# Relation rows in the first graph layer: from a per-edge gather to a one-hot matrix product

## The chip, the cores and the metric

The program runs on one core of one Trainium2 chip. Each core has TensorE (PE) for matrix products, VectorE (DVE), ScalarE (ACT), GpSimd (POOL), SyncE (SP), an on-chip memory of 128 partitions (SBUF), eight accumulation banks (PSUM) and sixteen DMA engines. The metric is device time in microseconds for one launch; lower is better.

## The reference

Two graph layers of a relational network and one graph transformer layer run over 50000 nodes and 25000 edges, all in float32 with 128 features. The change touches only the first of these layers:

```python
def _layer(h, e_h, src, dst, iso_mask, norm, W_r, W_sl, W_el):
    self_msg = jnp.where(iso_mask[:, None], h @ W_el, h @ W_sl)
    msg = (e_h + h[src]) @ W_r
    agg = jax.ops.segment_sum(msg, dst, num_segments=h.shape[0])
    return rrelu(agg * norm + self_msg)
...
e_h = rel_embed[rel_id]          # 25000 x 128, from a table of 200 rows
h = ent_embed
for W_r, W_sl, W_el in [(W_r1, W_sl1, W_el1), (W_r2, W_sl2, W_el2)]:
    h = _layer(h, e_h, src, dst, iso_mask, norm, W_r, W_sl, W_el)
```

The edges come sorted by `dst`. After the two layers follow a layer norm, an attention layer over the same edges and a feed-forward part over all nodes.

## The kernel before

The kernel is a row of stages, each a program of its own for every engine, with a barrier between two stages. `prepare` makes masks and index columns from the edge lists. `dense` runs over all nodes in 98 groups of 512 (NG = 98) and computes both layers for a node without edges; edges are corrected after it. `layer(0)` and `layer(1)` run over the edges in 49 groups of 512 (GE = 49), each of four tiles of 128 edges (GT = 4, T = 196 tiles). Then come `attention`, `softmax`, `weighted` and `ffn`.

Inside a stage every engine steps through the same counter `n`, and an operation with lag `a` works in step `n` on group `n - a`; semaphores do the rest. Each engine takes its instructions strictly in the order in which they are written.

**`dense`.** In step `n` SP issues the stores of older groups, then waits for the gather of pair `m = n - 5`, stores it to `edge_x` (L566), and only then loads `x_in` for group `n` (L571). POOL issues for each `m` two indirect DMAs of 128 rows of `x` (L538, `x_dst`, a ring of 8) and two of 128 rows of the relation table (L542) into `e_h`, a buffer of 196 tiles that stays in SBUF until the end of `layer(1)`. DVE does per step the two leaky maxima (L705, L756), the sum (L727), the norm's statistics, and its half of a search for the source positions (L689, every second step also L748). ACT evacuates PSUM (L647, L652, L657, L662), normalises three of four rows (L672) and counts signs (L637).

**`layer(0)`.** POOL gathers four tiles of source rows per group (L874, `h_src`, a ring of 6 groups). With A = 4, DVE first waits for all relation rows, then adds in step `n` the group's relation rows and source rows (`msg`, L955, group `n - 5`), takes the leaky maximum (L963, group `n - 8`), and alternates four `accT` (L1002, group `n - 6`) with four `mate` (L1011, group `n - 5`). PE does per step `p_acc` (L892, 4 products, group `n - 6`), `p_own` (L902, 4 transposes) and `p_h` (L911 and L912, 8 products, group `n - 7`). `layer(1)` gathers from `h1_table` and uses `e_h` directly as an operand of `p_acc` (L894).

Of the kernel before, what the change touches and what calls it, by code (L numbers as in the profile page):

```python
# [5 lines left out]
F32 = mybir.dt.float32  # L6
# [8 lines left out]
P = 128  # L15
# [12 lines left out]
SEG, FROM_PREV, TO_NEXT = range(3)  # L28
KINDS = 3
# [29 lines left out]
def gnn_program(nc, x, src, dst, edge_type_200, L0_gnn_rel_embed, L0_gnn_W_r1, L0_gnn_W_sl1, L0_gnn_W_el1,  # L59
# [18 lines left out]
    EDGES = GE * GROUP  # L78

# [11 lines left out]
    with root:  # L91
# [38 lines left out]
        types_in = sem("types_in", root)  # L130
# [36 lines left out]
        idx = sb("idx", [P, 6, T], I32)  # L167
        SRC, DST, AT_END, H_SRC, X_SRC, TYPE = range(6)
# [16 lines left out]
        def prepare():  # L185

            with ExitStack() as c:
# [14 lines left out]
                type_f = sb("type_f", [Q, W], F32, c)  # L202
# [54 lines left out]
                def _(e):  # L257
# [5 lines left out]
                    e.iota(row_id[:], pattern=[[1, 1]], base=0, channel_multiplier=1).then_inc(filled, 1)  # L263
                    e.memset(ident[:], 0.0).then_inc(consts, 1)
# [20 lines left out]
                def _(e):  # L285
                    e.wait_ge(filled, 6)
# [15 lines left out]
                    e.wait_ge(weights_in, 6 * 16)  # L302
# [20 lines left out]
                def _(e):  # L323
# [13 lines left out]
                    for n, t in enumerate((src_f, dst_in, end_f, seg_f, done_t, type_f)):  # L337
                        to_columns(n, t)
# [16 lines left out]
                def _(e):  # L355
# [13 lines left out]
                    e.tensor_copy(type_f[:], type_i[:])  # L369
# [77 lines left out]
                    e.wait_ge(turned, 6)  # L447
                    for n, t in ((0, idx[:, SRC, :]), (0, src_col[:]), (1, idx[:, DST, :]), (2, idx[:, AT_END, :]), (3, seg_col[:]), (5, idx[:, TYPE, :])):
# [10 lines left out]
                    e.wait_ge(turned, 7)  # L459
# [3 lines left out]
        def dense(e_h):  # L463

            XN, PN, SN = 16, 8, 4
            with ExitStack() as c:
# [67 lines left out]
                def _(e):  # L534
                    for m in range(NG):
# [246 lines left out]
        def layer(l, e_h):  # L782

            RN, HN, ON = 8, 6, 8
            with ExitStack() as c:
                rows = sb("rows", [P, RN, 2, 2 * W], U8, c)
                h_src = sb("h_src", [P, HN, GT, D], F32, c)
# [15 lines left out]
                p_h = [ps(f"p_h{s}", c) for s in range(2)]  # L803
                rows_in = sems("rows_in", RN, c)
# [20 lines left out]
                src_used = msg_ready if l == 0 else acc_prod  # L825
# [10 lines left out]
                def row_of(g, j, kind):  # L836
                    return tile_row(rows[:, g % RN, :, :], j, kind)

                @block.sync
                def _(e):  # L840
                    for n in range(STEPS):
# [7 lines left out]
                        if at_step(n, 0):  # L849
# [3 lines left out]
                            e.dma_start(rows[:, g % RN, :, :], edge_row(g, SEG, FROM_PREV + 1)).then_inc(rows_in[g % RN], 16)  # L853
# [15 lines left out]
                def _(e):  # L869
                    for g in range(GE):  # L870
                        wait(e, src_used, g - HN + 1)
                        for j in range(GT):
                            t = g * GT + j
                            e.indirect_dma_start(out=h_src[:, g % HN, j, :], out_offset=None, in_=(x, h1_table)[l],  # L874
                                                 in_offset=bass.IndirectOffsetOnAxis(ap=idx[:, (SRC, H_SRC)[l], t:t + 1], axis=0))\
# [3 lines left out]
                def _(e):  # L879
                    for n in range(STEPS):  # L880
# [23 lines left out]
                        if at_step(n, A + 3):  # L904
# [8 lines left out]
                            mm.then_inc(h_prod, 1)  # L913

                @block.scalar
                def _(e):
                    for n in range(STEPS):
                        if at_step(n, A + 2):
# [3 lines left out]
                            e.activation(ownT[:, g % 2, :], p_own[g % 2][:], ACT.Copy).then_inc(ownT_ready, 1)  # L922
                        if l and at_step(n, A + 8):
# [889 lines left out]
```

## Time and profile before

| | |
|---|---|
| median of 3 runs | 2668.84 us (2665.56 to 2669.47) |
| span of the profiled execution, first to last instruction | 2664.4 us |
| mean granted TensorE clock | 0.915 of full speed |
| instructions | 47955 |
| busy: PE, DVE, ACT, POOL | 2108.4, 1957.4, 1283.9, 1426.5 us |
| mean DMA rate | 159 GB/s |

The profiled execution's own time is not reported apart from its span: the span lies 1.2 us under the lowest and 5.1 us under the highest of the three runs, so between 1 and 5 us pass outside it. A busy share over the whole span mixes eight stages; the rows below are therefore cut by stage. `dense` runs from about 44 to 561 us, `layer(0)` from 564 to 830 us, `layer(1)` from 831 to about 1130 us, and `ffn` holds the last 740 us.

### The profile page before, as it was taken

Reading aid. Unit: us, or ns where it says so; the run is one execution under the profiler, and the core shown is the slowest. Engines: PE = TensorE matmul, PEld = TensorE weight load, DVE = VectorE, ACT = ScalarE, POOL = GpSimd, SP = SyncE. Lnnn points to the kernel's source line nnn. Section 1 sums busy time; section 2 is a strip of 40 time slices with the busy share of each in tenths; the row PEclk is TensorE's granted clock in tenths of the full one; section 3 lists DMA queues with packets and bytes.
Section 4 is the critical chain, followed back from the end, with each engine's and each line's share of the span. In section 5 each row is a group of like instructions: output and inputs, shape, how many; then the busy total and the mean of one; then the engine's idle time right before and its main releaser. Section 6 shows DMA issues by size and latency. Waiting matters only on the chain. (4 is left out here: it accounts for less than half of the span.)

```text
span 2664.4 us, 47955 instructions
## 1 busy us (share of the span) xinstructions
PE 2108.4 (79%) x13630; PEld 1693.7 (64%) x13630; DVE 1957.4 (73%) x7853; ACT 1283.9 (48%) x3019; POOL 1426.5 (54%) x1595
## 2 busy tenths in 40 slices
PE   3777777747776777669999607888299999999998
PEld 3555555537776777657777505666177777777776
DVE  4888888866665777878888685676377777777774
ACT  2788888842211444546565310000156666666665
POOL 2777777757775776275553004777533333333332
PEclk9899998878888999979999758999599999999999
DMA  3788888866666999744443005565313333333331
GB/s 90 218 247 243 240 241 238 239 191 181 180 177 186 298 292 290 231 137 128 124 122 108 30 0 152 177 194 188 148 60 108 108 103 109 105 106 107 106 105 51
DMA packets 378875, 423.36 MB, mean 159 GB/s; under 512 B 54686, under 2 KB 263274, under 8 KB 378614
## 3 DMA queue, kind: packets, MB, share of 16 engines
q1 hardware_dynamic: 334774, 337.16, 40.6%
q0 software_dynamic: 40768, 82.23, 11.8%
q8 instruction: 111, 1.82, 0.3%
q10 hardware_dynamic: 3072, 0.92, 0.2%
q14 instruction: 150, 1.23, 0.1%
HBM read 273.64 MB, written 179.87 MB: 170 GB/s over the span
## 5 line engine op out<-in xcount | busy, mean ns | idle before, releaser
L1670 PEld LDWEIGHTS p_y<-w,g_T 128*128 128x128 f32 x3136 | 365.4, 192 | 46.4 <-issue 24.2
L1670 PE MATMUL p_y<-w,g_T 128*128 128x128 f32 x3136 | 365.8, 275 | 0.0
L1653 POOL TENSOR_TENSOR rstd<-var,minus_half 128x4 f32<-128x4 f32 x98 | 113.5, 1159 | 450.3 <-ACT res L1701 450.2
L1663 PE MATMUL p_f<-nT,w 128*128 128x512 f32 x784 | 354.3, 595 | 0.0
L1688 ACT ACTIVATE nT<-p_n 128x512 f32<-128x512 f32 x98 | 58.5, 597 | 577.0 <-PE p_n L1678 577.0
L1695 ACT ACTIVATE g_T<-p_f,bf 128x512 f32<-128x512 f32 x392 | 267.1, 681 | 31.4 <-PE p_f L1663 31.3
L1083 POOL DMA_INDIRECT x_src<-x_rows,idx x196 | 185.1, 944 | 166.2 <-DVE normed L1250 73.6
L1488 POOL DMA_INDIRECT x_rows<-xv,idx x196 | 210.5, 1074 | 86.2 <-issue 53.1
L538 POOL DMA_INDIRECT x_dst<-in_x_dram,idx x196 | 197.1, 1005 | 100.5 <-issue 100.5
L874 POOL DMA_INDIRECT h_src<-h_table,idx x196 | 190.1, 970 | 87.7 <-issue 55.2
L1663 PEld LDWEIGHTS p_f<-nT,w 128*128 128x128 f32 x784 | 142.0, 191 | 141.7 <-issue 141.7
L874 POOL DMA_INDIRECT h_src<-in_x_dram,idx x196 | 190.5, 972 | 75.9 <-issue 58.8
L939 ACT ACTIVATE low<-p_h 128x512 f32<-128x512 f32 x98 | 58.5, 597 | 341.5 <-PE p_h L912 341.5
L542 POOL DMA_INDIRECT e_h<-in_L_gnn_rel_embed_dram,idx x196 | 187.0, 954 | 59.7 <-issue 59.7
L1717 DVE TENSOR_TENSOR xs<-p_y,xs 128x512 f32<-128x512 f32 x98 | 67.8, 692 | 184.8 <-PE p_y L1670 184.8
L1701 ACT ACTIVATE res<-xs,shift,rstd 128x128 f32<-128x128 f32 x392 | 189.3, 487 | 4.7 <-DVE shift L1756 4.7
L615 PE MATMUL p_r<-ident,h1T 128*128 128x128 f32 x392 | 67.1, 296 | 122.4 <-ACT h_rows L652 122.4
L911 PE MATMUL p_h<-w_r,accT 128*128 128x128 f32 x784 | 163.7, 293 | 0.0
L912 PE MATMUL p_h<-w_sl,ownT 128*128 128x128 f32 x784 | 161.4, 290 | 0.0
L608 PEld LDWEIGHTS p<-w_el,h1T 128*128 128x128 f32 x784 | 107.6, 203 | 71.9 <-DVE h1T L756 41.1
L1011 DVE TENSOR_SCALAR mate<-rows,seg_col,norm_col 128x128 f32<-128x128 uint8 x392 | 141.1, 363 | 10.2 <-DMA rows<-edge_rows 10.0
L1002 DVE SCALAR_TENSOR_TENSOR accT<-rows,accT,p_acc 128x128 f32<-128x128 uint8 x390 | 132.2, 339 | 12.6 <-PE p_acc L892 7.5
(298 smaller groups left out, 5683.5 us busy)
## 6 DMA issues: line engine op xcount, KB each, us to landing
xs<-x_rows SPq DMA_DIRECT2D x98, 512.0 KB, 3.6
x_in<-in_x_dram SPq DMA_DIRECT2D x98, 256.0 KB, 3.6
h_table<-h_rows SPq DMA_DIRECT2D x98, 256.0 KB, 3.9
x_rows<-x_in SPq DMA_DIRECT2D x98, 256.0 KB, 4.4
out_dram<-res SPq DMA_DIRECT2D x98, 256.0 KB, 2.1
x_rows<-x_rows SPq DMA_DIRECT2D x50, 500.0 KB
rows<-edge_rows SPq DMA_DIRECT2D x147, 128.0 KB, 4.5
edge_x<-x_dst SPq DMA_DIRECT2D x98, 128.0 KB, 2.2
```

The lines of the kernel that those rows point to most:

```text
L538: e.indirect_dma_start(out=x_dst[:, m % PN, j, :], out_offset=None, in_=x, in_offset=bass.IndirectOffsetOnAxis(ap=idx[:, DST, 2 * m + j:2 ...
L542: e.indirect_dma_start(out=e_h[:, t, :], out_offset=None, in_=L0_gnn_rel_embed, in_offset=bass.IndirectOffsetOnAxis(ap=idx[:, TYPE, t:t + ...
L874: e.indirect_dma_start(out=h_src[:, g % HN, j, :], out_offset=None, in_=(x, h1_table)[l], in_offset=bass.IndirectOffsetOnAxis(ap=idx[:, (S ...
L911: e.matmul(p_h[g % 2][:, at], accT[:, g % 2, at], w_r[l][:], start=True, stop=False)
L912: mm = e.matmul(p_h[g % 2][:, at], ownT[:, g % 2, at], w_sl[l][:], start=False, stop=True)
L1011: ins = e.tensor_scalar(mate[:, g % 2, j * P:(j + 1) * P], row_of(g, j, SEG), seg_col[:, t:t + 1], norm_col[:, t:t + 1], ALU.is_equal, ALU ...
L1083: e.indirect_dma_start(out=x_src[:, k % SN, j, :], out_offset=None, in_=x_rows, in_offset=bass.IndirectOffsetOnAxis(ap=idx[:, X_SRC, t:t + ...
L1488: e.indirect_dma_start(out=both_table.rearrange("n a d -> n (a d)"), in_=xv[:, g % VN, j, :, :].rearrange("p a d -> p (a d)"), in_offset=None,
L1663: e.matmul(p_f[ch][:], w_1[:, ch * P:(ch + 1) * P], nT[:, g % 2, :], start=True, stop=True).then_inc(f_prod, 1)
L1670: mm = e.matmul(p_y[g % 2][:, a * D:(a + 1) * D], g_T[:, g % 2, ch, a * P:(a + 1) * P], w_2[:, ch, :], start=(ch == 0), stop=(ch == FCH - 1))
L1695: e.activation(g_T[:, g % 2, ch, :], p_f[ch][:], ACT.Gelu, bias=bf1[:, ch:ch + 1]).then_inc(gelu_ready, 1)
L1701: ins = e.activation(res[:, g % RN, ch, :], xs[:, g % XN, ch, X1, :], ACT.Identity, scale=rstd2[:, g % 2, ch:ch + 1], bias=shift2[:, g % 2 ...
```

## The change

The relation rows are no longer gathered. `prepare` loads the table of 200 rows into SBUF (`rel`, two halves of 128 rows, the second padded with zeros) and writes each edge's type as a byte into `edge_rows`, as a fourth kind, instead of turning it into an index column. In `layer(0)` DVE compares the type bytes of 512 edges, spread over all partitions, with the row number of each partition, once for each half of the table (`onehot`, two instructions of 128x512). PE multiplies these with `rel` (8 products of 128x128 for a group) into two new PSUM banks `p_rel`. `msg` adds `p_rel` to the source rows, and ACT copies `p_rel` into `e_h`, which `layer(1)` needs.

The source rows of `layer(0)` are gathered into `e_h` itself, at the places which the relation rows take later, instead of into a ring of six groups. The first six groups' source rows (24 indirect DMAs) are gathered in `dense`; the other 43 groups' in `layer(0)`, up to 10 groups ahead of `msg`. The 196 relation gathers in `dense` are gone.

```diff
-SEG, FROM_PREV, TO_NEXT = range(3)
-KINDS = 3
+TYPE, SEG, FROM_PREV, TO_NEXT = range(4)
+KINDS = 4
...
+                    e.iota(rel_i[:], pattern=[[P, 2]], base=0, channel_multiplier=1).then_inc(filled, 1)
+                    e.memset(rel[:], 0.0).then_inc(filled, 1)
...
-                    e.wait_ge(filled, 6)
+                    e.wait_ge(filled, 8)
...
+                    e.dma_start(rel[:, 0, :], L0_gnn_rel_embed[0:P, :]).then_inc(weights_in, 16)
+                    e.dma_start(rel[0:RELS - P, 1, :], L0_gnn_rel_embed[P:RELS, :]).then_inc(weights_in, 16)
...
-                    e.tensor_copy(type_f[:], type_i[:])
+                    e.tensor_copy(rows[:, TYPE, :], type_i[:])
+                    e.tensor_copy(rel_id[:], rel_i[:])
...
-                    for n, t in ((0, idx[:, SRC, :]), (0, src_col[:]), (1, idx[:, DST, :]), (2, idx[:, AT_END, :]), (3, seg_col[:]), (5, idx[:, TYPE, :])):
+                    for n, t in ((0, idx[:, SRC, :]), (0, src_col[:]), (1, idx[:, DST, :]), (2, idx[:, AT_END, :]), (3, seg_col[:])):
...
-                        for t in (2 * m, 2 * m + 1):
-                            e.indirect_dma_start(out=e_h[:, t, :], out_offset=None, in_=L0_gnn_rel_embed,
-                                                 in_offset=bass.IndirectOffsetOnAxis(ap=idx[:, TYPE, t:t + 1], axis=0))\
-                                .then_inc(types_in, 16)
+                        if m < EARLY * GT:
+                            e.indirect_dma_start(out=x_src[:, m, :], out_offset=None, in_=x,
+                                                 in_offset=bass.IndirectOffsetOnAxis(ap=idx[:, SRC, m:m + 1], axis=0))\
+                                .then_inc(early_in, 16)
...
+            AHEAD = HN if l else 10
...
+                            if l == 0:
+                                wait(e, onehot_ready, g - RN + 1)
+                            e.dma_start(rows[:, g % RN, :, :], edge_row(g, FIRST, FROM_PREV + 1)).then_inc(rows_in[g % RN], 16)
...
+                    if l == 0:
+                        for g in range(EARLY, GE):
+                            k = g - EARLY
+                            if k >= AHEAD:
+                                e.wait_ge(msg_ready, g - AHEAD + 1)
+                            for t in range(g * GT, (g + 1) * GT):
+                                e.indirect_dma_start(out=e_h[:, t, :], out_offset=None, in_=x,
+                                                     in_offset=bass.IndirectOffsetOnAxis(ap=idx[:, SRC, t:t + 1], axis=0))\
+                                    .then_inc(gathered[k % AHEAD], 16)
+                        return
...
+                        if l == 0 and at_step(n, A):
+                            g = n - A
+                            e.wait_ge(onehot_ready, g + 1)
+                            wait(e, rel_ready, g - 1)
+                            for j in range(GT):
+                                at = slice(j * P, (j + 1) * P)
+                                for half in range(2):
+                                    mm = e.matmul(p_rel[g % 2][:, at], onehot[:, g % 2, half, at], rel[:, half, :],
+                                                  start=(half == 0), stop=(half == 1))
+                            mm.then_inc(rel_prod, 1)
...
+                        if l == 0 and at_step(n, A + 1):
+                            g = n - A - 1
+                            e.wait_ge(rel_prod, g + 1)
+                            e.wait_ge(msg_ready, g + 1)
+                            e.activation(e_h[:, g * GT:(g + 1) * GT, :].rearrange("p j d -> p (j d)"), p_rel[g % 2][:], ACT.Copy)\
+                                .then_inc(rel_ready, 1)
...
-                        e.wait_ge(types_in, 16 * T)
+                        e.wait_ge(early_in, 16 * EARLY * GT)
...
+                        if l == 0 and at_step(n, A):
+                            g = n - A
+                            e.wait_ge(rows_in[g % RN], 16 * (g // RN + 1))
+                            wait(e, rel_prod, g - 1)
+                            for half in range(2):
+                                ins = e.tensor_scalar(onehot[:, g % 2, half, :].rearrange("p (q i) -> p q i", q=2),
+                                                      rows[:, g % RN, :, 0:W], rel_id[:, half:half + 1], None, ALU.is_equal)
+                            ins.then_inc(onehot_ready, 1)
...
-                            e.wait_ge(gathered[g % HN], gathered.after(g % HN, GT * (g // HN + 1)))
+                            e.wait_ge(rel_prod, g + 1)
+                            if g >= EARLY:
+                                k = g - EARLY
+                                e.wait_ge(gathered[k % AHEAD], gathered.after(k % AHEAD, GT * (k // AHEAD + 1)))
...
-                            e.tensor_tensor(msg[:, g % 2, :, :].rearrange("p j d -> p (j d)"),
-                                            e_h[:, g * GT:(g + 1) * GT, :].rearrange("p j d -> p (j d)"),
-                                            h_src[:, g % HN, :, :].rearrange("p j d -> p (j d)"), ALU.add).then_inc(msg_ready, 1)
+                            e.tensor_tensor(msg[:, g % 2, :, :].rearrange("p j d -> p (j d)"), p_rel[g % 2][:],
+                                            e_h[:, g * GT:(g + 1) * GT, :].rearrange("p j d -> p (j d)"), ALU.add).then_inc(msg_ready, 1)
```

PE does its new products last in a step, DVE its new compares first. The `rows` DMA of `layer(0)` brings three kinds instead of two. `layer(1)` and all later stages keep their instructions.

## Rows read from the trace of the kernel before

**Rows 1.** The chain that ended last, by engine

```profile
PE 27%; DVE 0%; ACT 0%; DMA 0%; issue 0%; ACTq 0%
```

**Rows 2.** Busy us of each engine by stretch, mean granted clock, DMA share

```profile
core 0: us, PE busy (x) PEld busy (x) DVE busy (x) ACT busy (x) POOL busy (x), PEclk, DMA share, GB/s
44.00:556.00 512.00, 369.98 (x2548) 286.91 (x2548) 430.50 (x1958) 418.33 (x1170) 384.02 (x392) 0.92 0.79 234
100.00:500.00 400.00, 291.78 (x2025) 226.38 (x2026) 342.23 (x1560) 333.30 (x934) 305.22 (x312) 0.93 0.81 240
564.00:830.00 266.00, 191.46 (x1372) 184.37 (x1372) 165.87 (x490) 53.42 (x98) 190.53 (x196) 0.86 0.61 170
600.00:800.00 200.00, 151.19 (x1086) 146.34 (x1086) 131.38 (x391) 42.34 (x78) 152.19 (x157) 0.87 0.64 179
831.00:1130.00 299.00, 220.63 (x1764) 211.32 (x1764) 224.78 (x980) 135.78 (x339) 190.11 (x196) 0.93 0.91 279
2000.00:2300.00 300.00, 300.00 (x1782) 223.48 (x1782) 228.20 (x1008) 182.72 (x363) 106.07 (x161) 1.00 0.33 106
```

**Rows 3.** POOL's groups of instructions, 100 to 500 us: busy, mean ns, idle before

```profile
L538 POOL DMA_INDIRECT x_dst<-in_x_dram,idx x156 | 157.2, 1008 | 47.5 <-issue 47.5
L542 POOL DMA_INDIRECT e_h<-in_L_gnn_rel_embed_dram,idx x156 | 149.2, 957 | 47.5 <-issue 47.5
```

**Rows 4.** Waits of SP's queue, 100 to 500 us: us in total, times, longest

```profile
SPq L566 <- DMA x_dst<-in_x_dram,idx: 224.5, 73, 5.4
SPq L561 <- ACT x_in L672: 3.8, 4, 1.5
```

**Rows 5.** Waits of ACT, PE and DVE, 100 to 500 us

```profile
PE p_r L615 <- ACT h_rows L652: 106.0, 65, 4.1
ACT h_rows L652 <- DMA h_table<-h_rows: 57.6, 47, 3.2
DVE base L687 <- ACT junk L637: 20.1, 33, 1.7
DVE h L705 <- DVE junk L689: 17.5, 78, 0.6
DVE h1T L756 <- ACT low L657: 17.2, 18, 2.1
```

**Rows 6.** POOL's three groups of gathers, 44 to 830 us

```profile
L538 POOL DMA_INDIRECT x_dst<-in_x_dram,idx x196 | 197.1, 1005 | 100.5 <-issue 100.5
L874 POOL DMA_INDIRECT h_src<-in_x_dram,idx x196 | 190.5, 972 | 75.9 <-issue 58.8 <-POOLq L120 16.4 <-DVE msg L955 0.6
L542 POOL DMA_INDIRECT e_h<-in_L_gnn_rel_embed_dram,idx x196 | 187.0, 954 | 59.7 <-issue 59.7
```

**Rows 7.** The msg line L955 in the first layer: duration, first and last start, waits

```profile
L955 DVE TENSOR_TENSOR msg<-e_h,h_src x49: 678/693/766, 574.3 to 816.7; 128x512 f32<-128x512 f32 x49
its engine sat idle before it (us, times) until:
  DMA h_src<-in_x_dram,idx: 88.8, 30
```

**Rows 8.** Timeline of DVE, two steps at 300 us: start, us

```profile
299.99 0.69 DVE L705 TENSOR_TENSOR h<-low,p 128x512 f32<-128x512 f32 x1 [0.21 <-DVE junk L689]
302.63 0.65 DVE L748 TENSOR_SCALAR at_least<-srcs,first_col 98x512 bf16<-98x512 uint16 x2
304.89 0.69 DVE L705 TENSOR_TENSOR h<-low,p 128x512 f32<-128x512 f32 x1 [0.21 <-DVE junk L689]
```

**Rows 9.** Timeline of DVE at 542 us, a step without L748

```profile
542.52 0.69 DVE L705 TENSOR_TENSOR h<-low,p 128x512 f32<-128x512 f32 x1 [0.21 <-DVE junk L689]
...
546.78 0.69 DVE L705 TENSOR_TENSOR h<-low,p 128x512 f32<-128x512 f32 x1 [0.21 <-DVE junk L689]
```

**Rows 10.** DVE's L705, once for each of the 98 groups of the dense stage

```profile
L705 DVE TENSOR_TENSOR h<-low,p x98: 679/687/690, 58.4 to 549.4; 128x512 f32<-128x512 f32 x98
```

**Rows 11.** A float32 instruction of DVE at 128x512, in prepare

```profile
L456 DVE TENSOR_SCALAR w<-w,gcol x1: 481/481/481, 41.9 to 41.9; 128x512 f32<-128x512 f32 x1
```

**Rows 12.** Timeline of PE at 709 us; a float32 product is two records

```profile
709.15 1.06 PE L892 MATMUL p_acc<-mate,msg 128*128 128x128 f32 x8
710.04 0.60 PE L902 MATMUL p_own<-ident,h_own 128*128 128x128 f32 x4
710.48 0.28 PE L911 MATMUL p_h<-w_r,accT 128*128 128x128 f32 x1
```

**Rows 13.** Timeline of DVE, one step of the first layer without a wait

```profile
700.88 0.69 DVE L955 TENSOR_TENSOR msg<-e_h,h_src 128x512 f32<-128x512 f32 x1 [3.20 <-DMA h_src<-in_x_dram,idx]
701.50 0.68 DVE L963 TENSOR_TENSOR out_rows<-low,p_h 128x512 f32<-128x512 f32 x1
702.09 0.34 DVE L1002 SCALAR_TENSOR_TENSOR accT<-rows,accT,p_acc 128x128 f32<-128x128 uint8 x1
702.35 0.34 DVE L1011 TENSOR_SCALAR mate<-rows,seg_col,norm_col 128x128 f32<-128x128 uint8 x1
...
704.15 0.69 DVE L955 TENSOR_TENSOR msg<-e_h,h_src 128x512 f32<-128x512 f32 x1
```

**Rows 14.** The two-byte compare L748: shortest, median, longest ns

```profile
L748 DVE TENSOR_SCALAR at_least<-srcs,first_col x98: 322/347/551, 48.2 to 531.1; 98x512 bf16<-98x512 uint16 x98
```

**Rows 15.** The rows DMA, 556 to 700 us: issue, then time to landing

```profile
L853 SPq DMA_DIRECT2D rows<-edge_rows x31: 370/380/454, 563.8 to 695.7; - x31
DMA to landing us min/median/max: 3.1/4.6/6.8
```

**Rows 16.** SP's issues at the start of the first layer

```profile
563.79 0.39 SPq L853 DMA_DIRECT2D rows<-edge_rows  x1
564.23 0.46 SPq L856 DMA_DIRECT2D h_own<-edge_x  x1
```

**Rows 17.** Timeline of PE at 822 us, at the low clock

```profile
822.39 0.64 PE L912 MATMUL p_h<-w_sl,ownT 128*128 128x128 f32 x2
822.81 0.63 PE L911 MATMUL p_h<-w_r,accT 128*128 128x128 f32 x2
823.24 0.63 PE L912 MATMUL p_h<-w_sl,ownT 128*128 128x128 f32 x2
```

More of the change, by code:

```diff
@@ L78, in gnn_program @@
     EDGES = GE * GROUP
+    RELS = L0_gnn_rel_embed.shape[0]
+    assert P < RELS <= min(2 * P, BYTE)
+    EARLY = 6
     h1_table = nc.dram_tensor("h1_table", [N + EDGES, D], F32).ap()
@@ L166, in gnn_program @@
         bf2_rows = sb("bf2_rows", [P, D])
-        idx = sb("idx", [P, 6, T], I32)
-        SRC, DST, AT_END, H_SRC, X_SRC, TYPE = range(6)
+        idx = sb("idx", [P, 5, T], I32)
+        SRC, DST, AT_END, H_SRC, X_SRC = range(5)
+        rel = sb("rel", [P, 2, D])
+        rel_id = sb("rel_id", [P, 2])
         src_col = sb("src_col", [P, T])
@@ L336, in _ @@
                     e.wait_ge(cols_ready, 1)
-                    for n, t in enumerate((src_f, dst_in, end_f, seg_f, done_t, type_f)):
+                    for n, t in enumerate((src_f, dst_in, end_f, seg_f, done_t)):
                         to_columns(n, t)
@@ L458, in _, with dense @@
                     e.tensor_copy(att_bias[:], p_att[:, 0:D])
-                    e.wait_ge(turned, 7)
+                    e.wait_ge(turned, 6)
                     e.tensor_copy(by_half(done_col[:]), columns(4))
                     e.tensor_copy(by_half(norm_col[:]), columns(6))
-        def dense(e_h):
+        def dense(x_src):
             XN, PN, SN = 16, 8, 4
@@ L784, in layer @@
             RN, HN, ON = 8, 6, 8
+            FIRST = SEG if l else TYPE
+            AHEAD = HN if l else 10
             with ExitStack() as c:
-                rows = sb("rows", [P, RN, 2, 2 * W], U8, c)
-                h_src = sb("h_src", [P, HN, GT, D], F32, c)
+                rows = sb("rows", [P, RN, 2, (FROM_PREV + 1 - FIRST) * W], U8, c)
+                h_src = sb("h_src", [P, HN, GT, D], F32, c) if l else None
+                onehot = None if l else sb("onehot", [P, 2, 2, GROUP], F32, c)
                 h_own = sb("h_own", [P, HN, GT, D], F32, c)
@@ L803, in layer @@
                 p_h = [ps(f"p_h{s}", c) for s in range(2)]
+                p_rel = None if l else [ps(f"p_rel{s}", c) for s in range(2)]
+                onehot_ready = None if l else sem("onehot_ready", c)
+                rel_prod = None if l else sem("rel_prod", c)
+                rel_ready = None if l else sem("rel_ready", c)
                 rows_in = sems("rows_in", RN, c)
@@ L824, in layer @@
                 row_ready = sem("row_ready", c) if l else h_ready
-                src_used = msg_ready if l == 0 else acc_prod
                 block = program(c)
@@ L836, in row_of @@
                 def row_of(g, j, kind):
-                    return tile_row(rows[:, g % RN, :, :], j, kind)
+                    return tile_row(rows[:, g % RN, :, :], j, kind - FIRST)
                 @block.sync
@@ L869, in _ @@
                 def _(e):
+                    if l == 0:
[8 more added lines that the diff above has]
+                        return
                     for g in range(GE):
-                        wait(e, src_used, g - HN + 1)
+                        wait(e, acc_prod, g - HN + 1)
                         for j in range(GT):
                             t = g * GT + j
-                            e.indirect_dma_start(out=h_src[:, g % HN, j, :], out_offset=None, in_=(x, h1_table)[l],
-                                                 in_offset=bass.IndirectOffsetOnAxis(ap=idx[:, (SRC, H_SRC)[l], t:t + 1], axis=0))\
+                            e.indirect_dma_start(out=h_src[:, g % HN, j, :], out_offset=None, in_=h1_table,
+                                                 in_offset=bass.IndirectOffsetOnAxis(ap=idx[:, H_SRC, t:t + 1], axis=0))\
                                 .then_inc(gathered[g % HN], 16)
```

11 lines of the change are left out of this document (5 added, 6 removed).

## The prediction

> **What bounds the kernel now.** The chain that ended last is first, and it says little here: it follows PE through `ffn` for 27% of the span and stops there [rows 1]. All stages touched lie before it, behind barriers, so whatever they gain or lose reaches the end in full. I therefore read stage by stage.
>
> The second view is busy time by stretch [rows 2]. In `dense` no engine is full: over 400 us DVE is busy for 342.23, ACT for 333.30, POOL for 305.22 and PE for 291.78, DMA at 0.81. In the middle of `layer(0)` all are lower still. Busy shares alone name no bound.
>
> The third view does: POOL's groups. Its 312 gathers between 100 and 500 us take 157.2 + 149.2 us and sit idle for 47.5 + 47.5 us, all "issue", so POOL waited for nobody: 401.4 us of 400 [rows 3]. That stretch holds 78 steps, so four gathers cost 5.15 us a step, and that is the pace of the stage. The fourth view shows how it reaches the others: SP's queue waits 224.5 us, 2.9 us a step, for the `x_dst` gather [rows 4]. SP takes its work in order, so the `h1_table` stores stand behind that wait; ACT then waits 57.6 us for those stores before `h_rows`, and PE 106.0 us for ACT [rows 5]. The reader is to see a gather that nobody reads soon setting the pace of a stage through an in-order queue.
>
> `layer(0)` has the same bound: 196 gathers, 190.5 us busy and 58.8 us of issue, 1.27 us each, 5.09 us a group [rows 6]; `msg` waits 88.8 us for them, and its 48 intervals from 574.3 to 816.7 are 5.05 us each [rows 7].
>
> **Dense, part by part.** Removed are 196 gathers, 187.0 + 59.7 us of POOL's time [rows 6]; 24 are added. POOL's step falls from four gathers to two (2.6 us), or three in the first 24 steps (3.9 us). It stops being the bound. What is late next is DVE: 342.23 us over 78 steps is 4.39 us [rows 2], and 17.5 us over 78 is 0.22 us a step of a wait on its own chain, in every step [rows 5], which stays: 4.61 us. Single steps agree: 4.90 us with L748 [rows 8] and 4.26 us without it [rows 9], mean 4.58 us. DVE's other two waits, 20.1 and 17.2 us on ACT [rows 5], are 0.48 us a step. If they came only from SP's stall they go; if ACT's own order makes them they stay, and nothing is gained. The ends are 4.61 and 5.06 us; the latter is today's mean interval, (549.4 - 58.4) / 97 [rows 10]. ACT needs 333.30 / 78 = 4.27 us and PE 3.74 us [rows 2], both under DVE, and DMA gets 128 KB a step less. I take 4.65. Gain: 97 x (5.06 - 4.65) = **-40 us**; ends -44 and 0.
>
> **Prepare** gets an iota, a memset and two more loads, all small, ahead of or beside a chain that loses one column turn and one copy. The nearest duration is the 0.48 us of a DVE instruction over the same 512 columns [rows 11]; I take **+0.4 us**, ends 0 and 2.
>
> **The first layer, PE.** Today a group has 4 products of `p_acc` in 0.89 us and 4 transposes in 0.44 us [rows 12]; a product is 0.222 us, so the 8 of `p_h` are 1.78 us. That is 3.11 us. The change adds 8 products, 1.78 us: 4.89 us a group. This becomes the longest queue of the stage.
>
> **DVE.** A step without waits is 3.27 us [rows 13]. The two compares are not in the trace as such. Below, each could be as cheap as the two-byte compare of as many columns, 0.33 us when two follow each other [rows 8, 14]; a float32 scalar instruction of 512 columns is 0.48 us [rows 11]. Above, one element a cycle like `msg` gives 0.69 us [rows 7], and four times a byte-reading `mate` gives 4 x 0.26 = 1.04 us [rows 13]. I take 0.6, nearest to `msg`, because the byte-reading `mate` is no shorter than the byte-reading `accT` with three operands. DVE: 3.27 + 1.2 = 4.5 us, hidden behind PE's 4.89; ends 3.9 and 5.35. Only at the upper end would DVE bound, at 48 x 0.3 = +14 us over today.
>
> **Order of the loop.** The new waits are DVE's `msg` on `rel_prod`, behind which stand the maximum, four `accT` and four `mate`, and ACT's copy on `msg_ready`, behind which stands `low`. PE ends step `n - 1` with `p_rel`; then DVE does `msg` and everything after it in 3.27 us, and PE needs that `mate` only at the start of its next step, 4.89 us later. So 1.6 us of slack remains, and the next compare fills most of it. PE needs the compare only at the end of its step. ACT gains one copy of 0.6 us beside 53.42 us of work in 266 [rows 2]: nothing. It holds `low` for the next step, where it is due.
>
> **POOL** in this stage: 43 groups at 5.09 us, starting with the first six resident, some 30 us ahead of need, with room for ten. At 5.0 us a group the lead shrinks by 43 x 0.09 = 4 us: covered. `rows` grows by half, 64 KB a group, at a DMA share of 0.64 [rows 2], and is loaded over three steps ahead of its compare against 4.6 us to land [rows 15]: nothing.
>
> **Start and loop.** Today `msg` starts 10.5 us after SP's first issue [rows 7, 16], waiting for gathers. New: 4.6 us landing, 1.3 us compares, 8 products at the low clock, 0.428 us each [rows 17], 3.4 us: 9.3 us, **-1 us**. The loop: 4.89 plus 0.1 us for semaphores is 5.0 us, 48 x (5.0 - 5.05) = **-2.4 us**. PE starts cold: while it stays at the low clock a step costs 9.8 us; with one and a quarter such steps **+6 us** (ends 0 and 12). The drain behind the last `msg` keeps its work: 0.
>
> **The clock.** In `layer(0)` the granted clock was 0.87 in mean with PE busy for 151.19 of 200 us, in `layer(1)` 0.93, and in `ffn`, where PE never paused, 1.00 [rows 2]. Those are mixtures of the levels 1.2 and 2.4 GHz. I expect near 1.0 because PE becomes the bound and stops pausing. The Trainium skill, "TensorE: Matmul & The Clock Gate", section "HAM oscillation", warns of the opposite: bursts of products between waits keep falling back to the low clock. By it, were the pauses to remain, the loop would come out as the second rival; the 0.87 row bears that rule out for the present loop.
>
> **Sum.** -40 + 0.4 - 1 - 2.4 + 6 = -37 us. Against the profiled span of 2664.4 that is 2627.4; between 1 and 5 us lie around the span, so against the median of 2668.84 it is 2632 us.
>
> **Rivals.** *Dense is freed only in part.* ACT's and DVE's waits on each other stay, or the gathers and stores contend: 4.90 us a step, -16 us, sum -13, 2656 us. For it: 37.3 us of DVE's waits are on ACT [rows 5]. Against: ACT and PE were themselves waiting for SP, and free steps of 4.26 and 4.90 us exist.
>
> *PE bounds the first layer at a mixed clock.* At 0.87 the loop is 4.89 / 0.87 + 0.1 = 5.7 us, 48 x 0.65 = +31 us in place of -2.4, sum -4, 2665 us. For it: today's clock rows. Against: `ffn`.
>
> *Slower than before.* One mechanism: PE waits in each step for `mate`, because DVE waits in each step for `p_rel`, so the two alternate instead of overlapping. PE from `p_acc` to `p_rel` is 4.89 us, then DVE 3.27 us: 8.2 us a step if the lag of one step were no cover. It decides from 5.05 + (40 - 5) / 48 = 5.8 us on; halfway, 6.6 us, it is 48 x 1.55 = +74 us, sum +40, 2709 us. Against it stand the two-step lag and the slack worked out above; for it, that a cold PE (9.8 us) eats all slack once and may stay so.
>
> *It doesn't do what it says in dense*: SP would wait for the x_dst gather as long as now, because landing and not issue is slow. 0 us there, sum about +3, 2672 us. Against: POOL's issues fill the stretch to within 1.4 us.
>
> **Numbers.** Forecast 0.63, dense in part 0.13, mixed clock 0.12, alternation 0.06, no gain in dense 0.06. A measurement tells about 0.2%, 5 us, from no change. The mixed clock splits evenly between faster and same, and partly freed dense counts as faster. Faster 0.82, same 0.07, slower 0.11. The range goes from -54 (dense 4.58, no cold start, PE at 4.89) to -12, which takes in dense in part: 2615 to 2657.
>
> **What would show it.** In the new profile POOL should be idle for over 40% of `dense`, with SP waiting for ACT or DVE and no longer for `x_dst`; L705's intervals near 4.6 us; `layer(0)` with PE busy over 90% at a clock over 0.95, `msg` waiting for PE and not for DMA, intervals near 5.0 us; the compares 0.5 to 0.7 us each. The prediction is wrong if L705's intervals stay over 4.9 us, if the clock in `layer(0)` stays under 0.9, or if the compare takes over 0.85 us.

## The result, and the profile after

The changed kernel takes 2598.63 us (median of 4 runs, 2596.22 to 2603.09); the kernel before, run beside it, 2669.15 us (2665.56 to 2671.54). The ratio is 0.9742, with a 95% interval of 0.9729 to 0.9755: 70 us faster. Predicted were 37 us, with a range that ended at 54. The direction was right, the size about half.

The profiled execution has a span of 2594.5 us, 69.9 us less than before. The first view is busy time by stretch: the middle of `dense`, the middle of `layer(0)`, `layer(1)`.

```profile
core 0: us, PE busy (x) PEld busy (x) DVE busy (x) ACT busy (x) POOL busy (x), PEclk, DMA share, GB/s
100.00:450.00 350.00, 262.08 (x1997) 197.49 (x1996) 330.02 (x1538) 326.01 (x924) 173.21 (x175) 1.00 0.85 246
550.00:750.00 200.00, 200.00 (x1797) 200.00 (x1796) 170.81 (x489) 68.85 (x123) 136.56 (x141) 1.00 0.66 185
761.00:1060.00 299.00, 225.12 (x1764) 215.87 (x1764) 224.86 (x980) 135.53 (x339) 190.10 (x196) 0.91 0.92 279
```

Beside [rows 2], in the middle of `dense` DVE is now busy for 94% of the time (86% before) and POOL for 49% (76%). In the middle of `layer(0)` PE has no gap at all, and its granted clock, 0.87 before, is 1.00. `layer(1)` takes as long as it did.

The second view is POOL's groups and the waits of SP's queue, 100 to 450 us, beside [rows 3] and [rows 4].

```profile
L548 POOL DMA_INDIRECT x_dst<-in_x_dram,idx x165 | 163.3, 990 | 173.8 <-DMA edge_x<-x_dst 142.5 <-issue 31.3
...
SPq L571 <- ACT x_in L682: 150.3, 77, 2.9
```

POOL now waits 142.5 us for `x_dst` buffers to come free, so it runs ahead of SP; SP no longer waits for a gather but for ACT.

The third view is DVE's L715 (L705 before), once a group, beside [rows 10], and two steps of its timeline, beside [rows 8] and [rows 9].

```profile
L715 DVE TENSOR_TENSOR h<-low,p x98: 679/687/690, 59.7 to 497.3; 128x512 f32<-128x512 f32 x98
...
300.23 0.69 DVE L715 TENSOR_TENSOR h<-low,p 128x512 f32<-128x512 f32 x1 [0.21 <-DVE junk L699]
304.48 0.69 DVE L715 TENSOR_TENSOR h<-low,p 128x512 f32<-128x512 f32 x1 [0.21 <-DVE junk L699]
307.12 0.61 DVE L758 TENSOR_SCALAR at_least<-srcs,first_col 98x512 bf16<-98x512 uint16 x2
309.27 0.69 DVE L715 TENSOR_TENSOR h<-low,p 128x512 f32<-128x512 f32 x1 [0.21 <-DVE junk L699]
```

97 intervals fell from 491.0 to 437.6 us, 5.06 to 4.51 us each. Two lengths alternate: 4.26 us, and 4.79 or some 4.93 us in a step with the two-byte compare (L758, L748 before). The 0.21 us wait on DVE's own chain stands in each, and in these steps DVE has no other.

The fourth view is two DVE lines of `layer(0)`, `msg` beside [rows 7] and the new compare, then DVE's timeline over one step.

```profile
L1010 DVE TENSOR_TENSOR msg<-p_rel,e_h x49: 684/692/692, 518.3 to 750.1; 128x512 f32<-128x512 f32 x49
its engine sat idle before it (us, times) until:
  PE p_rel L949: 33.8, 48
...
L995 DVE TENSOR_SCALAR onehot<-rows,rel_id x98: 468/482/636, 513.5 to 744.0; 128x512 f32<-128x512 uint8 x98
...
601.37 1.02 DVE L995 TENSOR_SCALAR onehot<-rows,rel_id 128x512 f32<-128x512 uint8 x2
603.01 0.69 DVE L1010 TENSOR_TENSOR msg<-p_rel,e_h 128x512 f32<-128x512 f32 x1 [0.62 <-PE p_rel L949]
603.62 0.68 DVE L1017 TENSOR_TENSOR out_rows<-low,p_h 128x512 f32<-128x512 f32 x1
607.91 0.69 DVE L1010 TENSOR_TENSOR msg<-p_rel,e_h 128x512 f32<-128x512 f32 x1 [0.28 <-PE p_rel L949]
```

`msg` waits for `p_rel` in nearly every step, 33.8 us in all, and for no gather: PE is the bound. The 48 intervals of `msg` take 231.8 us (242.4 before). A compare is 0.48 us.

Where the 69.9 us went, each figure a difference of starts in the two traces, rounded: the 97 intervals of `dense` -53.4; its tail from the last L715 to SP's first issue in `layer(0)` -2.1 (14.4 to 12.3); that issue to the first `msg` -1.8 (10.5 to 8.7); the 48 intervals of `msg` -10.6; the drain behind them -1.6 (13.9 to 12.3); `prepare` +1.0; `dense`'s start +0.3; `layer(1)` -1.5; all behind it -0.1.

### The profile page after: what moved, and what is told of

It is laid out like the page before. It is cut to its first block and busy times, and to the rows that moved or that the text cites. A ratio compares the mean times of both kernels' runs of the same rounds, so it can differ in the third digit from the quotient of the medians.

```text
span 2594.5 us, 49618 instructions
## 1 busy us (share of the span) xinstructions
PE 2131.5 (82%) x14412; PEld 1724.0 (66%) x14412; DVE 1990.0 (77%) x7951; ACT 1308.9 (50%) x3068; POOL 1238.0 (48%) x1401
## 3 DMA queue, kind: packets, MB, share of 16 engines
q0 software_dynamic: 34496, 69.37, 10.6%
## 5 line engine op out<-in xcount | busy, mean ns | idle before, releaser
L618 PEld LDWEIGHTS p<-w_el,h1T 128*128 128x128 f32 x784 | 95.1, 191 | 188.7 <-DVE h1T L766 187.8
L894 POOL DMA_INDIRECT e_h<-in_x_dram,idx x172 | 166.8, 970 | 104.6 <-POOLq L123 52.5
L618 PE MATMUL p<-w_el,h1T 128*128 128x128 f32 x784 | 113.2, 287 | 109.2 <-DVE h1T L766 109.2
L939 PE MATMUL p_h<-w_r,accT 128*128 128x128 f32 x784 | 152.5, 276 | 0.0
L940 PE MATMUL p_h<-w_sl,ownT 128*128 128x128 f32 x784 | 152.2, 276 | 0.0
L922 PE MATMUL p_acc<-mate,e_h 128*128 128x128 f32 x392 | 88.3, 310 | 56.9 <-DVE mate L1065 52.7
```

What stands on the lines that cost most here:

```text
L618: mm = e.matmul(p_2[g % 2][:, a * D:(a + 1) * D], h1T[:, g % 2, a * P:(a + 1) * P], w_el[1][:], start=True, stop=True)
L939: e.matmul(p_h[g % 2][:, at], accT[:, g % 2, at], w_r[l][:], start=True, stop=False)
L940: mm = e.matmul(p_h[g % 2][:, at], ownT[:, g % 2, at], w_sl[l][:], start=False, stop=True)
```

## Experiments

The four of the first series ask what set the pace of `dense`: POOL's time for issuing, or the traffic of the relation gathers. The next four ask what sets the pace of `layer(0)`, and what the six early groups are worth. The last three follow from those. Each series ran beside the kernel before; ratios are to it, and the changed kernel stands at 0.9742. The pace is the mean over all 97 intervals of `dense` or all 48 of `msg`, the short first and last ones among them.

| run | median us | ratio, 95% | pace per step of the stage it changes |
|---|---|---|---|
| dense alone | 2608.59 | 0.9796 (0.9776 to 0.9816) | dense 4.51 |
| gathers put back | 2654.30 | 0.9963 (0.9946 to 0.9980) | dense 5.07 |
| POOL kept busy | 2640.16 | 0.9924 (0.9899 to 0.9950) | dense 4.92 |
| traffic alone | 2599.17 | 0.9764 (0.9744 to 0.9783) | dense 4.50 |
| products twice | 2685.24 | 1.0077 (1.0059 to 1.0095) | layer(0) 6.60 |
| products halved | 2587.20 | 0.9709 (0.9689 to 0.9730) | layer(0) 4.56 |
| one early group | 2609.12 | 0.9795 (0.9778 to 0.9813) | layer(0) 5.04 |
| twelve early groups | 2599.47 | 0.9757 (0.9739 to 0.9774) | layer(0) 4.83 |
| bf16, two parts, twelve | 2561.54 | 0.9604 (0.9588 to 0.9620) | layer(0) 4.04 |
| bf16, three parts, twelve | 2581.01 | 0.9674 (0.9658 to 0.9690) | layer(0) 4.45 |
| bf16, two parts, six | 2583.41 | 0.9688 (0.9671 to 0.9704) | layer(0) 4.57 |

### The dense stage alone

The kernel before, with its relation gathers replaced by a memset; `layer(0)` as before.

```diff
-                        for t in (2 * m, 2 * m + 1):
-                            e.indirect_dma_start(out=e_h[:, t, :], out_offset=None, in_=L0_gnn_rel_embed,
...
+                        e.memset(e_h[:, 2 * m:2 * m + 2, :], 0.0).then_inc(types_in, 1)
```

> The kernel before without its 196 relation gathers in dense; a GpSimd memset of e_h to zero (0.3 us a step) stands in for them, so the relation rows are left out of the result. The first layer keeps its own gathers. Theory P (GpSimd's issue of four gathers a step set the pace of dense): dense falls from 5.06 to 4.5 us a step as in the changed kernel, 55 us less, about 2614 us, and the first layer's msg intervals stay 5.05 us. Rival L (a good part of the 70 us belongs to the first layer and to what it leaves behind): over 2630 us.

```profile
L702 DVE TENSOR_TENSOR h<-low,p x98: 680/686/689, 60.6 to 498.1; 128x512 f32<-128x512 f32 x98
...
L952 DVE TENSOR_TENSOR msg<-e_h,h_src x49: 678/692/749, 521.0 to 762.6; 128x512 f32<-128x512 f32 x49
```

`dense` runs at 4.51 us a step, as in the changed kernel, and `layer(0)` at 5.03 us, as before the change. The ratio of 0.9796 is -54 us of 2662; the changed kernel's 0.9742 is -69. The forecast on record was -55 us. So some 54 us of the gain are the gathers gone from `dense`, and the new first layer, with its early gathers, brings the other 14 or so.

### Gathers put back, POOL kept busy, traffic alone

Three additions to the changed kernel, 172 times each in `dense`, so that a step holds four operations again: a gather into buffer space not yet in use; a small POOL arithmetic instruction of about the same length that moves nothing; a plain transfer of the same size on SP's queue.

```diff
+                            e.indirect_dma_start(out=x_src[:, t, :], out_offset=None, in_=x,
+                                                 in_offset=bass.IndirectOffsetOnAxis(ap=idx[:, DST, t:t + 1], axis=0))\
+                                .then_inc(extra_in, 16)
...
+                            e.tensor_tensor(x_src[:, t, 0:5], pw_in[:], pw_half[:], ALU.pow).then_inc(extra_in, 1)
...
+                                e.dma_start(x_src[:, t, :], x[t * P:(t + 1) * P, :]).then_inc(extra_in, 16)
```

> The changed kernel with 172 gathers of node rows added to dense, into tiles of e_h that are not yet in use, so that GpSimd issues four gathers in each step as before. Their rows are overwritten later and change no result. Theory P: dense back to 5.06 us a step, +53 us, about 2652 us, with the first layer's loop at 4.90 us. Rival T (traffic): the same, so this run only fixes the size that the next two must share out.

> The changed kernel with two power operations of 128x5 on GpSimd in each dense step (one in the first 24), which take its time without any DMA; their results are overwritten. From the 1.16 us of a 128x4 power in ffn I expect 1.3 us each. Theory P: two gathers at 1.25 and two powers at 1.3 are about 5.1 us a step, dense back near 5.06 us, 2645 to 2665 us. Rival T (the relation gathers cost by their DMA traffic): dense stays at 4.5 us, 2600 us.

> The changed kernel with the same number of transfers of the same size and packet length (128 rows of 512 bytes) added to dense, issued by SyncE's queue and not by GpSimd; their rows are overwritten. Theory P: dense stays at 4.5 us a step, 2600 us, at most 5 us more for 0.8 us of issue a step on SyncE. Rival T: dense back near 5 us a step, 2640 to 2655 us.

The intervals of the same DVE line, in this order:

```profile
L724 DVE TENSOR_TENSOR h<-low,p x98: 679/686/690, 60.7 to 552.1; 128x512 f32<-128x512 f32 x98
```

```profile
L728 DVE TENSOR_TENSOR h<-low,p x98: 676/686/689, 59.0 to 536.4; 128x512 f32<-128x512 f32 x98
```

```profile
L722 DVE TENSOR_TENSOR h<-low,p x98: 677/686/689, 60.0 to 496.6; 128x512 f32<-128x512 f32 x98
```

And POOL's groups of the second, 59 to 537 us:

```profile
L566 POOL TENSOR_TENSOR e_h<-pw_in,pw_half 128x5 f32<-128x5 f32 x170 | 204.4, 1209 | 2.3
L556 POOL DMA_INDIRECT x_dst<-in_x_dram,idx x190 | 195.5, 1029 | 46.2 <-issue 46.1
L560 POOL DMA_INDIRECT e_h<-in_x_dram,idx x22 | 21.2, 964 | 6.7 <-issue 6.7
```

The numbers of that view add up to 476 us of 478: POOL is full, and `dense` takes 4.92 us a step without one relation row being moved. That is less than the 5.07 us with gathers, and the run's 2640.16 us lie under the 2645 to 2665 expected: two powers of 1.21 us and two gathers of 1.27 us with their issue gap make about 4.96 us, not 5.1. In the same kernel SP's queue waits again for the `x_dst` gather, 189.6 us between 100 and 450 us. With the traffic and without POOL's work the pace is 4.50 us, at a DMA share of 0.91 in the middle of the stage. The added transfers differ from the gathers in two ways, they come from SP's queue and read rows that lie together; scattered reads without POOL's work were not run. With that said, the relation gathers cost `dense` their time on POOL, and the same number of bytes alone costs nothing that can be measured.

### Products twice, products halved

PE's new products are done twice (the result is the same), or for the first half of the table alone.

```diff
-                                for half in range(2):
-                                    mm = e.matmul(p_rel[g % 2][:, at], onehot[:, g % 2, half, at], rel[:, half, :],
-                                                  start=(half == 0), stop=(half == 1))
+                                for half in range(4):
+                                    mm = e.matmul(p_rel[g % 2][:, at], onehot[:, g % 2, half % 2, at], rel[:, half % 2, :],
+                                                  start=(half % 2 == 0), stop=(half % 2 == 1))
...
-                                for half in range(2):
-                                    mm = e.matmul(p_rel[g % 2][:, at], onehot[:, g % 2, half, at], rel[:, half, :],
-                                                  start=(half == 0), stop=(half == 1))
+                                mm = e.matmul(p_rel[g % 2][:, at], onehot[:, g % 2, 0, at], rel[:, 0, :],
+                                              start=True, stop=True)
```

> The changed kernel with the 8 products of p_rel done twice for each group, the second time over the first. Theory E (TensorE sets the first layer's pace now, its products back to back at 0.222 us): the step grows by exactly 8 x 0.222 = 1.78 us to 6.68 us, 48 x 1.78 = +85 us, about 2683 us against 2598. Rival V (VectorE or the hand-over between the two sets the pace): part of the new products fills TensorE's waiting, +40 to +65 us.

> The changed kernel with only the first half of the relation table in the products (4 instead of 8 for a group; edges of types 128 to 199 get a zero row, so the result is another). Theory E: TensorE's step falls to 4.0 us and GpSimd's gathers become the bound: 43 groups at 5.07 us from 510 us on, the last row lands near 731 us where the last msg now starts at 750, so -19 us, about 2580 us. Rival V: VectorE or the hand-over holds the step at 4.9 us, no change.

`msg` with the products twice, and halved:

```profile
L1010 DVE TENSOR_TENSOR msg<-p_rel,e_h x49: 691/692/693, 521.5 to 838.1; 128x512 f32<-128x512 f32 x49
its engine sat idle before it (us, times) until:
  PE p_rel L949: 123.5, 49
```

```profile
L1009 DVE TENSOR_TENSOR msg<-p_rel,e_h x49: 671/683/692, 517.3 to 736.3; 128x512 f32<-128x512 f32 x49
its engine sat idle before it (us, times) until:
  issue: 24.2, 15
```

Twice: the 48 intervals grow by 84.8 us, and from the third on each is 6.69 us, 1.79 more than 4.90, which is 8 products of 0.22 us. PE's queue is the pace, in full. Halved: the loop gives back 12.8 us, not the 45 x 0.85 = 38 that DVE's 4.05 us would allow, and less than the 19 expected. Fourteen steps, from the fourth on, run at 4.05 us, DVE's own length, as its timeline shows with no wait in a step:

```profile
550.31 0.87 DVE L994 TENSOR_SCALAR onehot<-rows,rel_id 128x512 f32<-128x512 uint8 x2
551.10 0.68 DVE L1009 TENSOR_TENSOR msg<-p_rel,e_h 128x512 f32<-128x512 f32 x1
...
554.36 0.87 DVE L994 TENSOR_SCALAR onehot<-rows,rel_id 128x512 f32<-128x512 uint8 x2
```

After them the lead of the gathers is used up and POOL sets the pace: its 172 gathers start from 510.0 to 732.9 us, 5.21 us for four, and the last `msg` starts at 736.3. The profile names the waits of `msg` only "issue"; that they end when a gather lands is read from these times. So three limits lie close together in this loop: POOL's gathers at 5.1 to 5.2 us, PE at 4.90, DVE at 4.05.

### One early group, and twelve

```diff
-    EARLY = 6
+    EARLY = 1
...
+    EARLY = 12
```

> The changed kernel with one group's source rows gathered in dense instead of six. Theory E: the first layer is bound by gathers again, 48 groups at 5.07 us, so its msg loop is about 240 us instead of 232 and starts some 2 us later, dense gains 1.5 us: together +7 us, 2605 us. Rival: the lead of six groups is worth nothing, 2598 us, or TensorE cools in its new pauses, +15 us or more.

> The changed kernel with twelve groups' source rows gathered in dense instead of six. Theory E: the first layer is TensorE's already, so nothing is gained there; 24 more dense steps run with three gathers, in which the changed kernel's pairs of steps took 9.19 us instead of 9.05, +1.7 us: 2600 us. Rival: the first layer still hangs on gathers somewhere, 5 us or more gained.

The middle of `layer(0)` with one early group, and `msg` with one and with twelve:

```profile
550.00:690.00 140.00, 135.73 (x1198) 134.07 (x1198) 114.36 (x332) 45.54 (x82) 106.77 (x110) 1.00 0.68 193
...
L1010 DVE TENSOR_TENSOR msg<-p_rel,e_h x49: 671/692/693, 516.8 to 758.5; 128x512 f32<-128x512 f32 x49
```

```profile
L1010 DVE TENSOR_TENSOR msg<-p_rel,e_h x49: 690/692/693, 519.8 to 751.4; 128x512 f32<-128x512 f32 x49
```

With one group the gathers pace the loop. POOL issues its 192 without a pause, 508.8 to 755.3 us, which is 5.16 us for four; the 48 intervals of `msg` are 5.04 us in the mean, since the first group lay ready. PE pauses now and then and the clock is still 1.00. Six groups of lead hide the difference, so they are worth some 8 us by the traces and 14 us by the ratios (7 were expected). Six more are worth nothing as long as PE needs 4.90 us.

### The one-hot matrix in bf16

The numbers 0 and 1 are exact in bf16. The table is split in `prepare` into two or three bf16 parts, whose products are summed in PSUM. A bf16 number holds 8 significant bits and a float32 24, so two parts keep some 16 bits and three can keep all. PE then does 16 or 24 bf16 products in place of 8 of float32.

```diff
-                onehot = None if l else sb("onehot", [P, 2, 2, GROUP], F32, c)
+                onehot = None if l else sb("onehot", [P, 2, 2, GROUP], BF16, c)
...
+                        chain(e.tensor_copy(rel_part[:, k, :, :], rel[:]))
+                        if k < PARTS - 1:
+                            chain(e.tensor_tensor(rel[:], rel[:], rel_part[:, k, :, :], ALU.subtract))
...
+                                    for k in range(PARTS):
+                                        mm = e.matmul(p_rel[g % 2][:, at], onehot[:, g % 2, half, at], rel_part[:, k, half, :],
+                                                      start=(half + k == 0), stop=(half == 1 and k == PARTS - 1))
```

> A version meant to be faster: the changed kernel with the one-hot matrix in bfloat16 and the relation table split into two bfloat16 parts (16 products for a group instead of 8; the relation rows keep about 16 bits), and twelve groups gathered in dense. Theory E: TensorE's step falls to about 4.0 us if a bfloat16 product of 128 columns takes a quarter of the float32 one (0.056 us), VectorE's step is the 4.05 us that the run with half the table showed, and gathers (37 groups at 5.07 us) end before the last msg: loop 48 x 4.06 = 195 us instead of 232, -37 us, prepare +1 us: about 2563 us. Rival: a product in bfloat16 costs over 0.11 us with its weight load, TensorE then stays the bound near 4.9 us and nothing is gained.

> As the run before with three bfloat16 parts (24 products for a group, relation rows to full float32 precision). Theory E: TensorE's step 3.11 + 24 x 0.056 = 4.45 us, loop 214 us, -18 us, prepare +1.5 us: about 2582 us. Rival as before: 24 products at 0.11 us make 5.8 us a step, +40 us.

> Two bfloat16 parts with only six groups gathered in dense. Theory E: the gathers are the bound again as with half the table, msg ends near 735 us, about 2586 us; so the twelve groups, which gained nothing with the float32 products, are worth some 20 us here. Rival: the lead is worth nothing here either, same time as with twelve.

Two parts with twelve early groups, `layer(0)` from 550 to 690 us and `msg`:

```profile
550.00:690.00 140.00, 139.98 (x1513) 139.41 (x1512) 139.77 (x415) 57.36 (x103) 106.58 (x105) 1.00 0.82 228
...
L1020 DVE TENSOR_TENSOR msg<-p_rel,e_h x49: 671/679/693, 518.8 to 712.9; 128x512 f32<-128x512 f32 x49
```

`msg` with three parts, and with two parts and six groups:

```profile
L1020 DVE TENSOR_TENSOR msg<-p_rel,e_h x49: 682/692/693, 521.2 to 734.6; 128x512 f32<-128x512 f32 x49
its engine sat idle before it (us, times) until:
  PE p_rel L959: 17.2, 44
```

```profile
L1020 DVE TENSOR_TENSOR msg<-p_rel,e_h x49: 671/680/692, 517.3 to 736.7; 128x512 f32<-128x512 f32 x49
```

With two parts DVE is busy for 139.77 of 140 us: it is the bound, at 4.05 us in most steps. With three parts PE bounds: from the fourth interval on each is 4.51 us. PE's timeline shows what the 24 products take, 602.26 to 603.61 us:

```profile
602.26 1.50 PE L959 MATMUL p_rel<-rel_part,onehot 128*128 128x128 bf16 x24
603.61 1.11 PE L929 MATMUL p_acc<-mate,msg 128*128 128x128 f32 x8
```

With six early groups the loop falls back on the gathers. The two edits are worth more together than apart: by the ratios twelve groups alone brought nothing (0.9757), the bf16 form alone some 14 us (0.9688), both some 37 us (0.9604). That kernel, at 2561.54 us, beats both kernels of this study; the one with three parts gives up 19 us of it for the full width of the table. How far the results of the two differ was not measured.

## Why the prediction was right or wrong

**The bound of `dense`: right, and shown.** That POOL's issuing paced the stage through SP's queue was read from [rows 3] and [rows 4]. Putting POOL's work back without traffic brings the slow pace back; putting the traffic back without POOL's work does not. DVE came next, as worked out.

**The size of `dense`: the term that failed first.** I took 4.65 us for each of 97 intervals, 451 us; they took 437.6, so -53.4 us came for -40. What failed is the sum 4.39 + 0.22 = 4.61 us, taken as what DVE needs, and its use on every interval. The 13.4 us come apart as follows.

The margin from 4.61 to 4.65 is 3.9 us, and had no reason. From 4.61 to the 4.58 of the single steps are 2.9 us. The single steps were right, since DVE's instructions take the same time before and after; here is one of them between 100 and 450 us, before first, and the compare, which is the one that differs:

```profile
L717 DVE BATCH_NORM_STATS2 stats<-x_in 128x6 f32<-128x128 f32 x276 | 58.0, 273 | 0.0
L748 DVE TENSOR_SCALAR at_least<-srcs,first_col 98x512 bf16<-98x512 uint16 x68 | 24.0, 393 | 0.0
...
L727 DVE BATCH_NORM_STATS2 stats<-x_in 128x6 f32<-128x128 f32 x308 | 64.8, 273 | 0.0
L758 DVE TENSOR_SCALAR at_least<-srcs,first_col 98x512 bf16<-98x512 uint16 x76 | 25.3, 374 | 0.0
```

DVE's busy time of 4.39 us a step held something of its waits. An instruction starts some 0.08 us before the recorded end of the one before it, as behind the `msg` at 603.01, but not behind a wait; so the 51 waits on ACT that went [rows 5] had lengthened the busy time too, by an estimated 0.05 us a step.

The largest part, 4.8 us, is none of DVE's. The first three and the last four intervals of `dense` take 27.1 us before and 27.2 us after, 3.9 us each, and I had put them at the full pace; the other 90 fell from 5.15 to 4.56 us.

The last 1.8 us are the compare. Its two instructions take 0.61 us together, or some 0.75, and I had taken a 4.90 us step with 0.65 [rows 8] for all of them. Between 60 and 480 us, 18 of 46 pairs after the change took 0.71 us or more, and in each of the 18 a POOL gather ended while the pair ran, as here; the 15 during which POOL did nothing took 0.61 us.

```profile
105.00 1.40 POOL L548 DMA_INDIRECT x_dst<-in_x_dram,idx  x1 [0.30 <-issue]
...
106.02 0.75 DVE L758 TENSOR_SCALAR at_least<-srcs,first_col 98x512 bf16<-98x512 uint16 x2
```

Before, 26 of 42 pairs were that long, and POOL was at work in all 42. So freeing POOL made DVE's own step a little shorter; by what means is not shown. The stage's tail gave 2.1 us more, which I had not counted.

**The cold start: a wrong sign.** I charged +6 us for PE at the low clock in the first steps. The step that failed is "a step costs 9.8 us", one and a quarter times: it took a full step's work. But `p_acc` and `p_h` lag behind `p_rel`, so the first steps are nearly empty. PE's timeline at the start of `layer(0)`:

```profile
514.52 3.78 PE L949 MATMUL p_rel<-rel,onehot 128*128 128x128 f32 x16 [19.12 <-DVE onehot L995]
518.09 1.06 PE L930 MATMUL p_own<-ident,h_own 128*128 128x128 f32 x4
518.94 2.23 PE L949 MATMUL p_rel<-rel,onehot 128*128 128x128 f32 x16
521.01 1.06 PE L920 MATMUL p_acc<-mate,msg 128*128 128x128 f32 x8
...
522.34 1.95 PE L949 MATMUL p_rel<-rel,onehot 128*128 128x128 f32 x16
```

The granted clock is 0.50 up to 519.5 us and 1.00 from 520 us on, before the first full step. At the low clock fall the first `p_rel` (3.78 us; the third takes 1.95), four transposes and a part of the second `p_rel`. By their starts that cost an estimated 2.5 us, of which the 1.8 of the first `p_rel` stood in the start's term already (3.4 us there). The first three intervals of `msg` are 2.88, 3.70 and 4.55 us, 3.6 us less than three of 4.90. Between +6 and -3.6 lie 9.6 us.

**The loop: right in kind, 4.6 us off.** PE bounds it, as forecast. The other 45 intervals are 4.90 us each: 20 products at 0.222 us and 4 transposes at 0.11 [rows 12] are 4.88; the 0.1 us for semaphores does not show in this queue, which is never empty. Together with the cold start that makes -10.6 us where the sum had +3.6.

**Small terms.** The start was -1.8 for -1. The drain was -1.6 for 0, and `layer(1)` with the stages behind it gave -1.6; no run isolated these. `prepare` with the start of `dense` cost 1.3 us for 0.4. So the 33 us missed are 13.4 + 2.1 in `dense`, 14.2 in the loop, 0.8 in its start, 1.6 + 1.6 behind it, less 0.9 (rounded).

**DVE in `layer(0)`: mis-sized, at no cost.** I priced a compare at 0.6 us, nearest to `msg`. It takes 0.48 us, the row of a float32 scalar instruction [rows 11], though it reads bytes, and the two add 0.79 us to the queue (550.31 to 551.10), not 1.2. The free step is 4.05 us against 4.5 worked out. That cost nothing here, since PE covers it, and it decides what the bf16 form is worth: with 4.5 us the best kernel would, by estimate, have lost 22 of the 38 us that its loop gains over the changed kernel's.

**The rivals.** Dense freed in part (4.90 us) and no gain in dense: the pace of 4.51 us refutes both. Mixed clock: the granted clock is 1.00 in the loop. The Trainium skill, "TensorE: Matmul & The Clock Gate", section "HAM oscillation", tells of a loop whose bursts of products are shorter than the waits between them and start at the low clock each time. The loop before had waits of up to 4.0 us between bursts of 3.4 to 9.2 us and fell back too (0.87), but the length of a pause alone did not decide it. Before, PE stopped for 2.44 us until 622.59 and then fell to the low clock; with the products halved it stopped for up to 2.61 us, 113.85 of 135 us busy, and the clock stayed at 1.00; with one early group for up to 1.7 us, also at 1.00. The rows are of before, then of the products halved:

```profile
623.50:626.50 3.00, 3.00 (x16) 3.00 (x15) 2.38 (x9) 0.00 (x0) 2.39 (x3) 0.50 0.97 276
```

```profile
600.00:735.00 135.00, 113.85 (x981) 110.61 (x980) 111.97 (x323) 44.57 (x81) 102.14 (x105) 1.00 0.64 183
```

What tells the two apart was not isolated. So a clock near 1.0 was forecast rightly, but PE may pause and still keep it. The alternation would have shown as `msg` and `p_acc` waiting in turn; only `msg` waits, 0.7 us a step, and doubling the products added their own length and no more.

**The range.** Its lower end, -54, took dense at 4.58 with no cold start. It shared the mistakes of the sum: all 97 intervals at one pace, no step shorter than those I had picked, though steps of 4.79 us with the compare stood in the trace of before too, no gain from a start with little work in it, and none behind the loop. The chances of the same time and of a slower kernel, 0.07 and 0.11, do not follow from the list before them either: half of the mixed clock and no gain in dense (+3 us, inside 5) are 0.12, the alternation 0.06.

## What to carry to other kernels

When a bound is removed, price the next one from single steps that ran free of it, not from busy time in the stretch that it congested. Look through all such steps for the shortest, count apart the steps at both ends of a stage, and let the range reach below the sum. Count an engine's issue time for gathers as work on an in-order queue: the same bytes from another queue cost nothing here, and an unrelated POOL instruction of nearly the same length cost 0.41 us a step where the gathers cost 0.56. In a pipeline with lags the first steps carry part of the work, so a cold clock costs a part of a step. And where three limits lie within some 1 us a step (about 5.1, 4.90 and 4.05 here), one edit alone brings little, and the pair that lifts two of them brings more than both apart.

## What the runs showed of the hardware

A compare from uint8 to float32 over 128x512 takes 0.48 us, as long as a float32 scalar instruction of that size and 0.2 us less than an addition of two float32 tiles (0.69 us). The float32 products of 128x128 follow each other every 0.222 us also through a loop that never pauses; 8 added ones cost 1.79 us. In bf16 the same product costs a quarter: 24 of them, each with its own weight load, take 1.35 us (602.26 to 603.61), 0.056 us each. POOL's power of 128x5 elements takes 1209 ns, nearly as much as a gather of 128 rows with its issue gap (1.27 us), which is why it could stand in for one. Two two-byte compares of 98x512 take 0.61 us beside an idle POOL and some 0.75 us when a gather of POOL's ends while they run.
